# Depthwise 5x5 convolution on TensorE: the corner tiles move both parts of their taps in one product

## The reference

```
k = jnp.transpose(kernel, (1, 2, 0))[:, :, None, :]
y = lax.conv_general_dilated(x, k, window_strides=(1, 1), padding='SAME',
        dimension_numbers=('NHWC', 'HWIO', 'NHWC'), feature_group_count=ch)
return x + y
```

## Time and profile before

| | |
|---|---|
| median of 3 runs | 820.39 us (820.22 to 821.93) |
| the profiled execution: its own time | 820.37 us |
| its span, first to last instruction | 818.6 us |
| PE busy | 805.5 us |
| DVE, ACT, POOL busy | 690.1, 624.1, 525.6 us |
| granted TensorE clock, mean | 1.00 |

### The profile page before, as it was taken

One profiled execution on the slowest core, in us unless ns is written; L12 is line 12 of the kernel. 1 busy time (PEld: TensorE's weight loads), 2 busy tenths in 40 slices (PEclk: granted clock), 3 DMA queues, 4 the chain that ended last, 5 costly groups with the idle time before them and its releaser, 6 DMA issues.

```text
span 818.6 us, 19135 instructions
## 1 busy us (share of the span) xinstructions
PE 805.5 (98%) x6912; PEld 805.4 (98%) x6912; DVE 690.1 (84%) x1828; ACT 624.1 (76%) x1442; POOL 525.6 (64%) x652
## 2 busy tenths in 40 slices
PE   5999999999999999999999999999999999999997
PEld 5999999999999999999999999999999999999997
DVE  6898888888888888888888888888888888888885
ACT  5777878787777778787777778787777777787775
POOL 7858566576665675756748566576565674756741
PEclk9999999999999999999999999999999999999999
DMA  9999999999999999999999999999999999999965
GB/s 357 426 426 408 375 381 363 383 368 385 368 370 389 364 381 376 375 381 364 378 377 379 386 368 370 377 376 378 382 361 382 372 386 376 368 376 376 381 261 229
DMA packets 28749, 304.43 MB, mean 372 GB/s; under 512 B 3184, under 2 KB 3312, under 8 KB 4208
## 3 DMA queue, kind: packets, MB, share of 16 engines
q1 hardware_dynamic: 28656, 303.22, 97.1%
HBM read 153.79 MB, written 149.42 MB: 370 GB/s over the span
## 4 chain that ended last, share of the span: by engine, by line
PE 98%; POOL 1%; DMA 0%; issue 0%; DVE 0%; ACT 0%; DVEq 0%
PE sums L380 33%; PE sums L383 33%; PE sums L382 33%; DMA first<-consts 0%; POOL matrix L263 0%; POOL spread L250 0%; POOL spare L238 0%; POOL taps L241 0%; POOL taps L236 0%; DVE y_out L333 0%; ACT y_out L292 0%; DVEq L132 0%
## 5 line engine op out<-in xcount | busy, mean ns | idle before, releaser
L380 PE MATMUL sums<-matrix,x_low 126*128 126x208 f32 (+5 forms) x2304 | 648.1, 281 | 8.3 <-POOL matrix L263 8.3
L383 PE MATMUL sums<-matrix,x_high 126*128 126x208 f32 (+5 forms) x2304 | 647.3, 281 | 0.0
L382 PE MATMUL sums<-matrix,x_high 126*128 126x208 f32 (+5 forms) x2304 | 646.3, 281 | 0.0
L292 ACT ACTIVATE y_out<-sums 128x270 f32<-128x270 f32 (+6 forms) x1152 | 443.4, 392 | 183.3 <-PE sums L383 179.5
L263 POOL TENSOR_TENSOR matrix<-spread,mask 127x300 fp32r<-127x300 f32 x384 | 338.5, 913 | 262.3 <-PE sums L383 262.1
L380 PEld LDWEIGHTS sums<-matrix,x_low 126*128 126x128 f32 (+1 forms) x2304 | 443.9, 193 | 8.2 <-POOL matrix L263 8.2
L383 PEld LDWEIGHTS sums<-matrix,x_high 126*128 126x128 f32 (+1 forms) x2304 | 444.3, 193 | 0.0
L382 PEld LDWEIGHTS sums<-matrix,x_high 126*128 126x128 f32 (+1 forms) x2304 | 444.2, 193 | 0.0
L333 DVE TENSOR_TENSOR y_out<-sums,y_out 128x120 f32<-128x120 f32 (+3 forms) x1344 | 295.5, 255 | 117.7 <-ACT y_out L292 113.8
L323 DVE TENSOR_TENSOR x_low<-x_in,x_high 128x768 fp32r<-128x768 f32 x384 | 379.8, 989 | 2.0 <-ACT x_high L285 2.0
L285 ACT ACTIVATE x_high<-x_in 128x768 fp32r<-128x768 f32 x288 | 239.8, 833 | 6.0 <-DMA x_in<-x 5.8
(11 more groups left out here) (4 smaller groups left out, 0.4 us busy)
## 6 DMA issues: line engine op xcount, KB each, us to landing
x_in<-x SPq DMA_DIRECT2D x95, 1536.0 KB, 9.9
y<-y_out SPq DMA_DIRECT2D x95, 1520.0 KB, 12.9
rest<-later SPq DMA_DIRECT2D x1, 2300.0 KB, 14.4
x_in<-x SPq DMA_DIRECT2D x4, 384.0 KB, 5.5
y<-y_out SPq DMA_DIRECT2D x1, 832.5 KB, 3.4
y<-y_out SPq DMA_DIRECT2D x1, 687.5 KB, 4.0
mask<-masks SPq DMA_DIRECT2D x1, 300.0 KB, 3.7
first<-consts SPq DMA_DIRECT2D x1, 125.0 KB, 2.1
```

The costliest lines, as they stand in the source:

```text
L292: act.activation(outputs(c, rows, cols), sums(c, t, rows, cols), ACT.Copy).then_inc(copied, 1)
L380: pe.matmul(target, low, turned[HIGH], start=tile is bank["tiles"][0], stop=False, skip_group_check=True)
L382: pe.matmul(target, high, turned[LOW], start=False, stop=False, skip_group_check=True)
L383: product = pe.matmul(target, high, turned[HIGH], start=False, stop=last, skip_group_check=True)
```

## The change

Four of the 24 tiles lie in the plane's corners (`CORNERS`: quarter 0 bank 0, quarter 1 bank 5, quarter 2 bank 8, quarter 3 bank 9). Their windows are 11 rows of 16 columns, so that two of them fit into a bank beside the neighbour tile: the bank's rows become 46 wide instead of 30 (`SPAN` + `EDGE`). For such a tile the two products with the high input become one with 2 x 11 x 16 = 352 moving columns: the high taps' window goes to the cells as before, the low taps' window to cells 30 further on, the low sums. DVE adds the low sums to the output plane in an add of their own, 176 elements, after the bank's seams. `cast_high` is gone: ACT makes all four high pieces, and the tables are changed.

```diff
+CORNERS = ((0, 0), (2, 0), (2, 1), (0, 1))
+SPAN = 2 * LONG + HALO
+EDGE = LONG + HALO
...
-HIGH_AFTER = (2, 5, 7)
-CAST_AFTER = 2
-LOW_AFTER = (4, 5, 7, 9)
+HIGH_AFTER = (1, 3, 5, 7)
+LOW_AFTER = (4, 6, 7, 9)
...
+            row, k = CORNERS[quarter]
+            corner = k if n == row else None
...
+                              deep=short[1] - short[0], pitch=SPAN + EDGE * (corner is not None)))
...
+        if bank["corner"] is not None:
+            cells_of_corner = bank["corner_cells"]
+            after = [n + 1 for n, e in enumerate(earlier) if meet(e, cells_of_corner)]
+            bank["adds"].append((cells_of_corner, after[-1] if after else 0, LOW))
+            earlier.append(cells_of_corner)
...
+        def low_sums(c, t):
+            plane = plane_of(c, t)[:, :, SPAN:SPAN + EDGE]
+            return plane.rearrange("p x y -> p y x") if PLAN[t]["kind"] == TALL else plane
+
+        def both_sums(window, wide):
+
+            return bass.AP(tensor=window.tensor, offset=window.offset,
+                           ap=[window.ap[0], [SPAN - wide[0], 2], window.ap[1], window.ap[2]])
...
-            for piece in range(1, PIECES):
+            for piece in range(PIECES):
                 split_high(0, piece)
...
-                        split_high(c + 1, HIGH_AFTER.index(t) + 1)
+                        split_high(c + 1, HIGH_AFTER.index(t))
...
-                dve.tensor_copy(x_high[c % SLOTS][:, cols], x_in[c % X_SLOTS][:, cols]).then_inc(cast_done, 1)
...
-                    dve.tensor_tensor(y, sums(c, t, rows, cols), y, ALU.add).then_inc(added, 1)
+                    terms = sums(c, t, rows, cols) if part == HIGH else low_sums(c, t)
+                    dve.tensor_tensor(y, terms, y, ALU.add).then_inc(added, 1)
...
-                        if t == CAST_AFTER:
-                            cast_high(c + 1)
...
-                        pe.matmul(target, high, turned[LOW], start=False, stop=False, skip_group_check=True)
-                        product = pe.matmul(target, high, turned[HIGH], start=False, stop=last, skip_group_check=True)
+                        if bank["corner"] is not None and tile is bank["tiles"][bank["corner"]]:
+                            product = pe.matmul(both_sums(target, wide), high, turned, start=False, stop=last,
+                                                skip_group_check=True)
+                        else:
+                            pe.matmul(target, high, turned[:, LOW], start=False, stop=False, skip_group_check=True)
+                            product = pe.matmul(target, high, turned[:, HIGH], start=False, stop=last,
+                                                skip_group_check=True)
```

More of the change, by code:

```diff
@@ L79, in banks_of_plane @@
                     from_row=short[0] - (v - HALO), from_col=a - (u - HALO)))
-            banks.append(dict(quarter=quarter, kind=kind, rows=rows, cols=cols, tiles=tiles,
-                              deep=short[1] - short[0], pitch=long[1] - long[0]))
+            row, k = CORNERS[quarter]
+            corner = k if n == row else None
+            banks.append(dict(quarter=quarter, kind=kind, rows=rows, cols=cols, tiles=tiles, corner=corner,
+                              deep=short[1] - short[0], pitch=SPAN + EDGE * (corner is not None)))
+            if corner is not None:
+                across_it = tuple(long[0] + w for w in tiles[corner]["wide"])
+                banks[-1]["corner_cells"] = (rows, across_it) if kind == FLAT else (across_it, cols)
     return banks
@@ L113, in plan_of_sums @@
             after = [n + 1 for n, e in enumerate(earlier) if meet(e, seam)]
-            bank["adds"].append((seam, after[-1] if after else 0))
+            bank["adds"].append((seam, after[-1] if after else 0, HIGH))
             earlier.append(seam)
+        if bank["corner"] is not None:
[3 more added lines that the diff above has]
+            earlier.append(cells_of_corner)
         covered |= cells
@@ L161, in build @@
         taps_step, spread_step, matrix_step = sem("taps_step"), sem("spread_step"), sem("matrix_step")
-        cast_done, high_ready, low_ready = sem("cast_done"), sem("high_ready"), sem("low_ready")
+        high_ready, low_ready = sem("high_ready"), sem("low_ready")
         sums_done, copied, added = sem("sums_done"), sem("copied"), sem("added")
@@ L301, in _ @@
                     if c + 1 < CHANNELS and t in HIGH_AFTER:
-                        split_high(c + 1, HIGH_AFTER.index(t) + 1)
+                        split_high(c + 1, HIGH_AFTER.index(t))
         @block.vector
         def _(dve):
[L306 to L314, removed]
-                dve.tensor_copy(x_high[c % SLOTS][:, cols], x_in[c % X_SLOTS][:, cols]).then_inc(cast_done, 1)
             def split_low(c, piece):
                 cols = piece_cols(piece)
[L319 to L322, removed]
+                dve.wait_ge(high_ready, PIECES * c + piece + 1)
                 dve.tensor_tensor(x_low[c % SLOTS][:, cols], x_in[c % X_SLOTS][:, cols],
@@ L326, in add_seams @@
             def add_seams(c, t):
-                for n, ((rows, cols), after) in enumerate(PLAN[t]["adds"]):
+                for n, ((rows, cols), after, part) in enumerate(PLAN[t]["adds"]):
                     if n == 0:
@@ L337, in _ @@
                 dve.memset(y_out[slot][:, PLANE:OUT_COLS], 0.0).then_inc(pads_zeroed, 1)
-            cast_high(0)
             for piece in range(PIECES):
@@ L375, in _ @@
                         high, low = x_high[c % SLOTS][0:pixels, images], x_low[c % SLOTS][0:pixels, images]
-                        turned = [matrix[c % SLOTS][kind][0:pixels, part, :].rearrange("p (r q) -> p r q", q=COLS)[
-                            :, tile["from_row"]:tile["from_row"] + deep,
-                            tile["from_col"]:tile["from_col"] + wide[1] - wide[0]] for part in (HIGH, LOW)]
+                        turned = matrix[c % SLOTS][kind][0:pixels, :, :].rearrange("p h (r q) -> p h r q", q=COLS)[
+                            :, :, tile["from_row"]:tile["from_row"] + deep,
+                            tile["from_col"]:tile["from_col"] + wide[1] - wide[0]]
                         last = tile is bank["tiles"][-1]
-                        pe.matmul(target, low, turned[HIGH], start=tile is bank["tiles"][0], stop=False,
+                        pe.matmul(target, low, turned[:, HIGH], start=tile is bank["tiles"][0], stop=False,
                                   skip_group_check=True)
-                        pe.matmul(target, high, turned[LOW], start=False, stop=False, skip_group_check=True)
-                        product = pe.matmul(target, high, turned[HIGH], start=False, stop=last, skip_group_check=True)
+                        if bank["corner"] is not None and tile is bank["tiles"][bank["corner"]]:
[5 more added lines that the diff above has]
+                                                skip_group_check=True)
                     product.then_inc(sums_done, 1)
```

## The result

The changed kernel takes 805.82 us (median of 4 runs, 805.59 to 806.26) against 820.52 us of the kernel before (4 runs in the same comparison); the ratio is 0.9818, with a 95% interval of 0.9801 to 0.9835. The forecast was 806.2 us. The total came out, but two of its terms did not: they were off by 7 and 9 us and nearly cancelled.

A forecast was written before the change was run, and what follows sets the result against it. PE's stream was taken to bound the kernel: 0.88 us removed less 0.732 added saves 0.148 us a plane, x 96 = 14.2 us, so 820.37 - 14.2 = 806.2 us; DVE, ACT and transfers cost nothing. Range 792 to 813.5 us.

The forecast's parts named there:

- What bounds: Whole kernel: PE's stream of 805.5 us sets the time, with 8.3 us of start and 4.8 us of tail.
- Pairs removed: PE, four corner tiles: two products at 0.22 us a pair go away, 0.88 us a plane.
- Added: one product of 22 rows of 16: PE, corner tiles: merged product costs 202 ns in banks 0 and 5, 164 in 8 and 9; 0.732 us a plane.
- the floor: PE: small windows all cost 0.103 to 0.113 us each, however many columns, taken for the weight load.
- the saved weight load itself gives nothing more than the two floors already counted: PE, merged products: one weight load fewer brings no further saving, as the floor (0.11) is far below.
- its own signs: Wrong if PE waits in mid-stream, merged products are off 0.20 and 0.16 us, or all products beside them change price.
- The rival by columns: PE's merged products: one column a cycle, 147 ns each, saving 28.0 us, so 792.4 us; chance 0.14.
- The line rule that stood beside the forecast: SBUF reads: crossing 16-byte lines costs; 4/5 of 202 = 162 ns for column-0 windows, saving 14.6 us.
- The rival that every row costs 9.2 ns: PE's merged products: four of 202 ns, saving 0.072 us a plane, 6.9 us, so 813.5 us; chance 0.17.
- priced at nothing: DVE: cast gone (0.90 us), four adds come (1.00); 7.42 us of an 8.24 us plane, hidden behind PE.
- The rival that DVE binds: DVE's corner adds: cost time from 0.455 us each; at 0.55, 22 us slower, 842 us; chance 0.03.
- ACT and the transfers: ACT: one more high piece, 7.22 of 8.24 us, costs nothing; loads and stores at 384 GB/s have room.

The follow-up runs named there:

- The shifted matrices: The changed kernel with its matrices lying 8 bytes further on and nothing else changed; 802.03 us, ratio 0.9771 to the kernel before.
- the tables alone: The changed kernel with the merge switched off, keeping the new tables and all four high pieces on ACT; 820.54 us, ratio 0.9997 to the kernel before.

## Why the prediction came out as it did

**What bounds: right.** PE's stream set the time before and sets it after, and undoing the merge alone gives the old time back. The plane was sized a little long: 8.39 us is PE's busy time over 96, with a first plane of 10.5 us in it, while later planes took 8.37 from start to start; so the 8.24 us that were to be seen came out as 8.20.

**Pairs removed: right.** 0.88 us were read from two of the four pairs; the means of the four add up to 0.887.

**"Added: one product of 22 rows of 16": mis-sized.** 0.732 us were forecast for the four, 0.804 measured, 6.9 us over the run. The price of a row was right: 9.2 forecast and 9.0 to 9.1 measured, 7.45 (164 / 22) and 7.2 to 7.6. The second was luck in part: 164 is the middle of two bounds, and the lower one stands for the price by columns, which the runs rule out. What failed is pricing a product as rows times price and nothing else. Some 9 ns a product in banks 0 and 5 and some 30 in banks 8 and 9 come on top, and 193 ns lies above the 181 that the forecast gave as its upper end. Of the 30 ns, the floor might hold part, since the low product ahead takes only 95 to 98 ns, less than the floor, and could leave the rest to the merged one. The shifted matrices speak against a plain handing-on: there the low products ahead of the cheap merged ones take only 84 to 87 ns, and the merged ones 191 to 193 all the same. What the 30 ns are stays open.

**What the sum left out.** "the saved weight load itself gives nothing more than the two floors already counted": wrong. The product behind a merged one costs 92 ns less a plane, 8.9 us over the run. With 4 rows in place of 11 this is lost again, and with 8 in place of 11 it is kept, so it is the long product that gives it: behind one of 150 ns and more, 11 rows of 18 take 98 to 104 ns, which is their price by rows. A floor that is kept over two products together fits this; why the products behind banks 8 and 9 took 128 and 151 ns before, more than the floor and more than their rows, no run shows.

**How close the total came: luck.** The forecast saving of 14.2 us, less 6.9 for the merged products, plus 8.9 for the products behind them, plus 0.6 for the pairs, less 1.1 for all others (11 ns a plane), is the 15.7 us of the steady planes, of which the early planes took away 2.0 and the start gave back 0.8. By its own signs the prediction was wrong in part: the merged product was off 0.16 in banks 8 and 9, and the products behind the four changed their price.

**Columns or rows.** The rival by columns (147 ns each) is out: 9.1 ns for a row of 16 columns is 1.8 columns a ns where 147 ns needs 2.4, and the same 16 columns cost 7.4 ns from another start. With it goes, for such short rows in float32r, the rule by columns of the Trainium skill (TensorE: Matmul & The Clock Gate, Back-to-back issue gap), which that section gives for a matmul by itself: it makes 149 ns where 192 to 211 were measured. The line rule that stood beside the forecast (SBUF — State Buffer, section Door 1: The DMA port swizzle of the Trainium skill) is borne out by the shift of 8 bytes: four lines against five, 7.4 / 9.1 = 0.81. The rival that every row costs 9.2 ns is out as well, though its sum for the four, 0.808 us, was nearer than mine; without the saving behind it, it gave 813.5.

**DVE: hidden but for 1.0 us, and its plane mis-sized.** It was priced at nothing, and early waits cost 1.0 us. Its plane was forecast at 7.42 us and is 0.935 x 8.20 = 7.67. From 100 to 700 us, DVE is busy 85.5% of a plane of 8.37 us before and 77.1% with the tables alone, so the cast gave 0.70 us and not 0.90; without the low adds it is busy 81.3% of 8.20, so they cost 1.00 and not 1.16. And a low piece has become longer, 1046 ns in the mean instead of 989, which is 0.23 us a plane. Rows of DVE and POOL at one moment show where:

```profile
404.64 0.95 DVE L330 TENSOR_TENSOR x_low<-x_in,x_high 128x768 fp32r<-128x768 f32 x1
...
406.44 1.64 DVE L330 TENSOR_TENSOR x_low<-x_in,x_high 128x768 fp32r<-128x768 f32 x1
```

```profile
405.64 3.93 POOL L284 TENSOR_TENSOR matrix<-spread,mask 127x300 fp32r<-127x300 f32 x4 [2.23 <-PE sums L392]
```

The low piece beside POOL's matrix work takes 1.64 us, the one just ahead of it 0.95. The Trainium skill (SBUF — State Buffer, section SBUF: two separate sides) says that a DVE operation with two inputs in SBUF and a GpSimd operation that reads SBUF share a port which one holds for a whole instruction; the trace agrees: low pieces with no work of POOL beside them take 949 ns in the mean, the others 1078. The adds are not the reason, though. Low pieces in the runs with the tables alone and without the low adds:

```profile
L330 DVE TENSOR_TENSOR x_low<-x_in,x_high 128x768 fp32r<-128x768 f32 x384 | 378.6, 986 | 5.8 <-ACT x_high L306 5.3
...
L325 DVE TENSOR_TENSOR x_low<-x_in,x_high 128x768 fp32r<-128x768 f32 x384 | 403.9, 1052 | 6.2 <-ACT x_high L301 5.9
```

They take 986 ns with the old plane's length, and 1052 with the new one though no add was made. What changed is the last piece of a plane: with the new length it takes over 1.1 us in 26% of the planes, and in 31% without the adds; before and with the tables alone it does so in none. How it comes to fall on POOL's work there is not shown. POOL's products went from 913 to 1027 ns, most of it (997) with the tables alone. The rival that DVE binds was some 0.3 us a plane away, by the estimate above.

**ACT and the transfers: right.** ACT is at 85% where 88 was forecast, the transfers at 382 GB/s where 384 was; they rose from 377 at the same DMA share of 1.00, which was indeed no sign of a limit.

## What to carry to other kernels

Price a product from start to start by its shape, and then together with its neighbours: here over half of the saving was in the instruction behind the one that changed. When the moving operand has short rows, look at where they start; 8 bytes were worth 4 us, without an instruction more or less. And a forecast that hits the total deserves the same look at its terms as one that misses.

## What the runs showed that was not expected

- A product may cost less than the floor (82 to 89 ns against 110) if the next one then costs more; a price read from one matmul is not a floor until its neighbour is read too.
- The same 14 rows of 16 columns cost 0.13 us from one start and 0.11 from another 8 bytes on, and rows of 18 columns cost the same from both.
- DVE at 97.4% was full: 0.23 us of each plane stayed unused even when PE waited for it in every plane.
- Making PE's plane shorter made DVE's low pieces longer, from 986 to 1052 ns, with no add of DVE's more or less.
